# Tridiagonal reduction of a 512 x 512 matrix on one core: reordered steps for three and four remaining tiles, filled pauses for one

## The reference, cut to what matters

```
deg = sum(A, 0) + sum(A, 1) - diagonal(A);  d = rsqrt(deg)
L_norm = d[:, None] * (diag(deg) - A) * d[None, :]
_, U = eigh(L_norm)
h = relu(einsum('mn,bnd->bmd', U.T, x) @ W1 + b1)
x = layernorm(x + einsum('nm,bmd->bnd', U, h @ W2 + b2))
```

## Time and profile before

| | |
|---|---|
| runs (us) | 4988.99, 4991.18, 4991.94; median 4991.18 |
| profiled execution: time, span (us) | 4989.5, 4987.7 |
| busy, share of span | PE 51%, weight load 35%, VectorE 81%, ScalarE 23%, GpSimd 6% |
| the 510 steps | first next column (L1096) at 58.9 us, last at 2530.4 us |
| chain that ended last | VectorE 68%, TensorE 21%, issue 7%, ScalarE 2% |

### The profile page before, as it was taken

One profiled execution on the slowest core, in us unless ns is written; L12 is line 12 of the kernel. 1 busy time (PEld: TensorE's weight loads), 2 busy tenths in 40 slices (PEclk: granted clock), 3 DMA queues, 4 the chain that ended last, 5 costly groups with the idle time before them and its releaser, 6 DMA issues.

```text
span 4987.7 us, 116618 instructions
## 1 busy us (share of the span) xinstructions
PE 2551.1 (51%) x40168; PEld 1721.1 (35%) x40168; DVE 4026.5 (81%) x24921; ACT 1139.3 (23%) x5016; POOL 284.9 (6%) x1424
## 2 busy tenths in 40 slices
PE   4666666555556666544457645657423223135048
PEld 3444444444445555433322212322122223124024
DVE  7666666777777888888889999999967897988956
ACT  1212222222223333333311143333210200301001
POOL 1111111111110000000000000000000000000000
PEclk6555555555555555555567767778755555557579
DMA  2000000000000000000000000000000000000001
GB/s 69 2 2 2 2 2 2 2 2 2 2 2 3 4 4 4 3 3 2 3 1 1 1 1 1 1 1 1 1 1 0 0 0 0 0 0 1 0 0 34
DMA packets 20961, 20.11 MB, mean 4 GB/s; under 512 B 6544, under 2 KB 16784, under 8 KB 20368
## 3 DMA queue, kind: packets, MB, share of 16 engines
...
## 4 chain that ended last, share of the span: by engine, by line
DVE 68%; PE 21%; issue 7%; ACT 2%; SPq 0%; DVEq 0%; DMA 0%; POOL 0%
PE bank L622 10%; DVE qp L1437 2%; DVE hid L1096 2%; DVE dif L1799 2%; PE bank L593 2%; PE bank L617 2%; DVE pcol L1076 2%; DVE tau_row L1084 2%; DVE qp L1424 2%; DVE gated L1082 2%; DVE ts L1040 1%; DVE yz L1055 1%; ACT ts L358 1%; DVE hid L1085 1%; PE bank L783 1%
## 5 line engine op out<-in xcount | busy, mean ns | idle before, releaser
L622 PE MATMUL bank<-lapw,hid 128*32 128x160 f32 (+3 forms) x10200 | 660.0, 420 | 81.5 <-DVE lapw L1105 58.3
L622 PEld LDWEIGHTS bank<-lapw,hid 128*32 128x32 f32 x10200 | 394.3, 162 | 200.0 <-DVE lapw L1105 79.7
L700 PE MATMUL bank<-hid,rows 128*128 128x512 f32 (+1 forms) x504 | 320.1, 802 | 275.3 <-ACT dif L410 271.9
L586 PE MATMUL bank<-xp,ones 128*32 128x1 f32 x4080 | 146.0, 202 | 458.1 <-DVE xp L1070 240.6
L371 ACT ACTIVATE swap<-vcols 128x4 f32<-128x4 f32 (+3 forms) x510 | 105.7, 207 | 1049.4 <-DVE xp L1070 696.8
L1050 DVE TENSOR_TENSOR yz<-bank,pick 128x128 f32<-128x128 f32 (+3 forms) x510 | 117.6, 231 | 233.7 <-PE bank L622 233.5
L700 PEld LDWEIGHTS bank<-hid,rows 128*128 128x128 f32 x504 | 118.7, 242 | 468.1 <-ACT dif L410 297.2
L586 PEld LDWEIGHTS bank<-xp,ones 128*32 128x32 f32 x4080 | 102.6, 140 | 501.4 <-DVE xp L1070 262.2
L593 PE MATMUL bank<-ycol,vcols 128*32 128x1 f32 x3064 | 89.8, 199 | 236.3 <-DVE ycol L1061 236.3
L593 PE MATMUL bank<-hid 128*32 128x1 f32 x3064 | 89.8, 199 | 191.6 <-DVE hid L1096 191.6
L586 PE MATMUL bank<-xn,ones 128*32 128x2 f32 x4080 | 141.2, 198 | 84.1 <-DVE xn L1009 84.1
...
## 6 DMA issues: line engine op xcount, KB each, us to landing
...
hid<-pair SPq DMA_DIRECT2D x32, 1.0 KB, 1.7
...
dif<-in_L_gnn_Wih SPq DMA_DIRECT2D x1, 0.5 KB, 7.1
```

The lines of the kernel that those rows point to most:

```text
L586: m = pe.matmul(into[32 * q:32 * q + 32, :], weights, column, start=True, stop=True)
L622: m = pe.matmul(bank[1][32 * q:32 * q + 32, 0:(T + 1) * 32].rearrange("p (u i) -> p u i", i=32), acols[:, t, k:k + 1].to_broadcast([P, 32] ...
L700: m = pe.matmul(bank[4 * h + q][:, 0:cols_], wih_t[:, p - 1, q * P:(q + 1) * P], hid[:, b0:b0 + nb, t:t + (nw - 1) * p + 1:p], start=True, ...
```

## The change

`dots(k)` becomes two functions, `gated_early(k)` (three or four tiles) and `direct(k)` (one or two); they are each other's opposite.

- Three and four tiles: on VectorE gate_row, gated, tau_row, scrow and ats are issued ahead of the copy of the product (L1050) instead of behind pcol; L1093's product is issued behind bcol_. On TensorE the tail's sum is issued inside the strips, behind the second tile, instead of behind the panel's row. The panel's factor (L1103) is issued ahead of norms(k+1), whose first instruction no longer counts in norm_in.
- One tile: the two instructions on the product are issued behind L1040, and the panel's slots (L1058) behind the second of `pair`.
- All: L1040 waits for the reciprocal (L1037) instead of for L1038, and with one or two tiles the reciprocal is ahead of the wait for alpha. pcol counts in pcol_ready, for which ScalarE waits ahead of w0 and TensorE ahead of the last sum. `product` has its loops exchanged, the tiles outside.

On GpSimd only a branch that no step takes (`t0 == NT - 1`) goes; `tiny` moves in the list of buffers. The core of the diff, ScalarE, TensorE, then VectorE (indented less here):

```
     act.wait_ge(p_ready, k + 1)
-    if dots(k):
+    if direct(k):
         act.activation(ts[:, 7:8], tau_row[:, k:k + 1], ACT.Copy, scale=0.5)
+    act.wait_ge(pcol_ready, k + 1)
     act.activation(w0[:, t0:], pcol[:, t0:], ACT.Copy, scale=tau_row[:, k:k + 1]).then_inc(w0_ready, 1)
...
 def product(into, left, right):
-    for q in range(4):
-        for t in range(T):
+    for t in range(T):
+        for q in range(4):
             m = pe.matmul(into[32 * q:32 * q + 32, :], left[:, t:t + 1].to_broadcast([P, 32]), right[:, t:t + 1], start=(t == 0), stop=(t == T - 1))
...
+    early = gated_early(k)
+    if early:
+        pe.wait_ge(norm_in, k + 1)
+        everywhere(bank[0][:, 0:2], ones[:, 0:32], xn[:, 0:2]).then_inc(norm_ps, 1)
+    else:
         pe.wait_ge(a_ready, k + 1)
         product(bank[0][:, 0:1], acols[:, t0:, k], acols[:, t0:, k]).then_inc(norm_ps, 1)
         everywhere(bank[5][:, 0:1], unit(k), acols[:, t0, k:k + 1]).then_inc(alpha_ps, 1)
-    else:
-        pe.wait_ge(norm_in, 2 * (k + 1))
-        everywhere(bank[0][:, 0:2], ones[:, 0:32], xn[:, 0:2]).then_inc(norm_ps, 1)
...
+        if t == t0 + 1 and early:
+            pe.wait_ge(tail_in, k + 1)
+            everywhere(bank[4][:, 0:1], ones[:, 0:32], xn[:, 2:3]).then_inc(tail_ps, 1)
     m.then_inc(y_done, 1)
     if j:
         everywhere(bank[2][:, 0:2 * j], unit(k), lapw[:, t0, N:N + 2 * j]).then_inc(rowz_ps, 1)
     if k:
         pe.wait_ge(vy_saved, k)
-    pe.wait_ge(tail_in, k + 1)
-    if dots(k):
+    if not early:
+        pe.wait_ge(tail_in, k + 1)
         product(bank[4][:, 0:1], sq[:, 0, t0:], sq[:, 0, t0:]).then_inc(tail_ps, 1)
-        pe.wait_ge(x_ready, k + 1)
+    pe.wait_ge(x_ready, k + 1)
+    if direct(k):
         product(bank[3][:, 0:1], vcols[:, t0:, k], ycol[:, t0:]).then_inc(vy_ps, 1)
-        pe.wait_ge(x2_ready, k + 1)
+        pe.wait_ge(pcol_ready, k + 1)
         product(bank[2][:, 4 * NB:4 * NB + 1], vcols[:, t0:, k], pcol[:, t0:]).then_inc(vp_ps, 1)
     else:
-        everywhere(bank[4][:, 0:1], ones[:, 0:32], xn[:, 2:3]).then_inc(tail_ps, 1)
-        pe.wait_ge(x_ready, k + 1)
         everywhere(bank[3][:, 0:1], ones[:, 0:32], xp[:, 0:1]).then_inc(vy_ps, 1)
         pe.wait_ge(x2_ready, k + 1)
         everywhere(bank[2][:, 4 * NB:4 * NB + 1], ones[:, 0:32], xp[:, 1:2]).then_inc(vp_ps, 1)
...
     dve.wait_ge(a_ready, k + 1)
-    V.tensor_tensor(xn[:, 1:2], acols[:, t0, k:k + 1], ident[:, e:e + 1], ALU.mult).then_inc(norm_in, 1)
+    V.tensor_tensor(xn[:, 1:2], acols[:, t0, k:k + 1], ident[:, e:e + 1], ALU.mult)
     V.tensor_tensor_reduce(jcol[:, 0, t0:], a, a, 1.0, 1e-32, ALU.mult, ALU.add, xn[:, 0:1]).then_inc(norm_in, 1)
...
+    def strips():
+
+        dve.wait_ge(y_done, k + 1)
+        at = put(V.tensor_tensor(yz[:, t0:, 0:32], bank[1][:, 0:T * 32].rearrange("p (t i) -> p t i", i=32),
+                                 pick[:].unsqueeze(1).to_broadcast([P, T, 32]), ALU.mult))
+        if j:
+            dve.wait_ge(w2_ready, k)
+            dve.wait_ge(v2_ready, k)
+            at = put(V.tensor_tensor(yz[:, t0:, 32:32 + 2 * j], panel_cols(j, t0), panel_rows(bank[1][:, T * 32:T * 32 + 32], j, T), ALU.mult))
+        return at
+
+    def slots():
+
+        dve.wait_ge(rowz_ps, rowz)
+        return put(V.tensor_tensor(tz[:, t0:, 1:1 + 2 * j], panel_cols(j, t0), panel_rows(bank[2], j, T), ALU.mult))
+
+    if j:
+        rowz += 1
     dve.wait_ge(norm_root, k + 1)
-    if dots(k):
+    a = put(V.reciprocal(ts[:, 3:4], ts[:, 0:1]))
+    if not early:
         scalars += 1
         dve.wait_ge(alpha_ps, scalars)
-    put(V.reciprocal(ts[:, 3:4], ts[:, 0:1]))
-    a = put(V.tensor_scalar(ts[:, 1:2], alpha, 0.0, 0.5, ALU.is_ge, ALU.subtract))
+    put(V.tensor_scalar(ts[:, 1:2], alpha, 0.0, 0.5, ALU.is_ge, ALU.subtract))
     after(a)
     a = put(V.tensor_scalar(ts[:, 4:5], ts[:, 3:4], bank[0][:, 0:1], ts[:, 0:1], ALU.mult, ALU.add))
+    if T == 1:
+        z = strips()
     after(a)
     a = put(V.tensor_tensor(pair[:, k, 0:1], ts[:, 4:5], ts[:, 1:2], ALU.mult))
     b = put(V.scalar_tensor_tensor(pair[:, k, 1:2], ts[:, 4:5], ts[:, 1:2], alpha, ALU.mult, ALU.add))
+    if T == 1 and j:
+        c = slots()
     after(a)
-    vdone = put(V.scalar_tensor_tensor(v, onehot[:, t0:, k + 1], pair[:, k, 0:1], a_, ALU.mult, ALU.add))
+    put(V.scalar_tensor_tensor(v, onehot[:, t0:, k + 1], pair[:, k, 0:1], a_, ALU.mult, ALU.add))
     after(b)
-    put(V.reciprocal(inv[:], pair[:, k, :]))
-
-    dve.wait_ge(y_done, k + 1)
-    a = put(V.tensor_tensor(yz[:, t0:, 0:32], bank[1][:, 0:T * 32].rearrange("p (t i) -> p t i", i=32),
-                            pick[:].unsqueeze(1).to_broadcast([P, T, 32]), ALU.mult))
-    if j:
-        dve.wait_ge(w2_ready, k)
-        dve.wait_ge(v2_ready, k)
-        a = put(V.tensor_tensor(yz[:, t0:, 32:32 + 2 * j], panel_cols(j, t0), panel_rows(bank[1][:, T * 32:T * 32 + 32], j, T), ALU.mult))
-        rowz += 1
-        dve.wait_ge(rowz_ps, rowz)
-        c = put(V.tensor_tensor(tz[:, t0:, 1:1 + 2 * j], panel_cols(j, t0), panel_rows(bank[2], j, T), ALU.mult))
-    after(a)
-    if dots(k):
-        V.tensor_reduce(ycol[:, t0:], yz[:, t0:, 0:32 + 2 * j], AX.X, ALU.add).then_inc(x_ready, 1)
+    d = put(V.reciprocal(inv[:], pair[:, k, :]))
+    if early:
+        dve.wait_ge(tail_ps, k + 1)
+        g = put(V.tensor_scalar(gate_row[:, k:k + 1], bank[4][:, 0:1], 1e-24, -1.0, ALU.is_gt, ALU.mult))
+        after(g)
+        g = put(V.tensor_scalar(gated[:], inv[:], gate_row[:, k:k + 1], None, ALU.mult))
+        after(g)
+        V.tensor_tensor(tau_row[:, k:k + 1], gated[:, 0:1], gated[:, 1:2], ALU.mult).then_inc(p_ready, 1)
+        dve.wait_ge(p_ready, k + 1)
+        g = put(V.tensor_scalar(scrow[:, k:k + 1], tau_row[:, k:k + 1], gated[:, 0:1], -1.0, ALU.mult, ALU.mult))
+        after(g)
+        put(V.scalar_tensor_tensor(ats[:, t0:], a_, scrow[:, k:k + 1], ltm[:, t0:, k + 1], ALU.mult, ALU.mult))
+    if T > 1:
+        z = strips()
+        if j:
+            c = slots()
+    after(z)
+    y = V.tensor_reduce(ycol[:, t0:], yz[:, t0:, 0:32 + 2 * j], AX.X, ALU.add)
+    if direct(k):
+        y.then_inc(x_ready, 1)
     else:
-        y = put(V.tensor_reduce(ycol[:, t0:], yz[:, t0:, 0:32 + 2 * j], AX.X, ALU.add))
+        y = put(y)
     if j:
         after(c)
     dve.wait_ge(edge_ready, k + 1)
     a1done = put(V.tensor_reduce(a1[:, t0:], tz[:, t0:, 0:1 + 2 * j], AX.X, ALU.add))
-    if not dots(k):
-        after(max(y, vdone))
+    if not early:
+        dve.wait_ge(tail_ps, k + 1)
+        g = put(V.tensor_scalar(gate_row[:, k:k + 1], bank[4][:, 0:1], 1e-24, -1.0, ALU.is_gt, ALU.mult))
+    if not direct(k):
+        after(y)
         V.tensor_tensor_reduce(jcol[:, 1, t0:], v, ycol[:, t0:], 1.0, 0.0, ALU.mult, ALU.add, xp[:, 0:1]).then_inc(x_ready, 1)
-    dve.wait_ge(tail_ps, k + 1)
-    g = put(V.tensor_scalar(gate_row[:, k:k + 1], bank[4][:, 0:1], 1e-24, -1.0, ALU.is_gt, ALU.mult))
     after(a1done)
     if k:
         dve.wait_ge(w0_ready, k)
-    p = V.scalar_tensor_tensor(pcol[:, t0:], a1[:, t0:], pair[:, k, 0:1], ycol[:, t0:], ALU.mult, ALU.add)
-    if dots(k):
-        p.then_inc(x2_ready, 1)
-    else:
-        put(p)
-    after(g)
-    g = put(V.tensor_scalar(gated[:], inv[:], gate_row[:, k:k + 1], None, ALU.mult))
-    after(g)
-    V.tensor_tensor(tau_row[:, k:k + 1], gated[:, 0:1], gated[:, 1:2], ALU.mult).then_inc(p_ready, 1)
+    V.scalar_tensor_tensor(pcol[:, t0:], a1[:, t0:], pair[:, k, 0:1], ycol[:, t0:], ALU.mult, ALU.add).then_inc(pcol_ready, 1)
+    if not early:
+        after(max(d, g))
+        g = put(V.tensor_scalar(gated[:], inv[:], gate_row[:, k:k + 1], None, ALU.mult))
+        after(g)
+        V.tensor_tensor(tau_row[:, k:k + 1], gated[:, 0:1], gated[:, 1:2], ALU.mult).then_inc(p_ready, 1)
+    dve.wait_ge(pcol_ready, k + 1)
     b = put(V.scalar_tensor_tensor(bcol_[:, t0:, k + 1], pcol[:, t0:], gated[:, 0:1], a1[:, t0:], ALU.mult, ALU.add))
-    dve.wait_ge(p_ready, k + 1)
-    c = put(V.tensor_scalar(scrow[:, k:k + 1], tau_row[:, k:k + 1], gated[:, 0:1], -1.0, ALU.mult, ALU.mult))
+    if not early:
+        dve.wait_ge(p_ready, k + 1)
+        c = put(V.tensor_scalar(scrow[:, k:k + 1], tau_row[:, k:k + 1], gated[:, 0:1], -1.0, ALU.mult, ALU.mult))
+    if not direct(k):
+        V.tensor_tensor_reduce(jcol[:, 2, t0:], v, pcol[:, t0:], 0.5, 0.0, ALU.mult, ALU.add, xp[:, 1:2]).then_inc(x2_ready, 1)
     after(b)
     b = put(V.tensor_tensor(bm[:, t0:], bcol_[:, t0:, k + 1], ltm[:, t0:, k + 1], ALU.mult))
-    after(c)
-    c = put(V.scalar_tensor_tensor(ats[:, t0:], a_, scrow[:, k:k + 1], ltm[:, t0:, k + 1], ALU.mult, ALU.mult))
-    if not dots(k):
-        V.tensor_tensor_reduce(jcol[:, 2, t0:], v, pcol[:, t0:], 0.5, 0.0, ALU.mult, ALU.add, xp[:, 1:2]).then_inc(x2_ready, 1)
-    after(c)
+    if not early:
+        after(c)
+        b = put(V.scalar_tensor_tensor(ats[:, t0:], a_, scrow[:, k:k + 1], ltm[:, t0:, k + 1], ALU.mult, ALU.mult))
```

(33 more changed lines are left out.)

19 lines of the change are left out of this document (8 added, 11 removed).

## The result

The changed kernel takes 4878.5 us (median of four runs, 4876.9 to 4878.8), the kernel before 4991.6 us in the same comparison: ratio 0.9773, 95% interval 0.9756 to 0.979. That is 113 us less, where 124 were forecast; 4867 was the forecast, 4838 to 4912 its range. The profiled execution has a span of 4876.7 us against 4987.7, 111 us less.

A forecast was written before the change was run, and what follows sets the result against it. With three or four tiles the product's end was taken to bind, with two and one VectorE's dependent instructions. 79 + 5 + 8 + 32 = 124 us off 4989.5, plus 1.7 for the median, gave 4867 us, range 4838 to 4912.

The forecast's parts named there:

- (a) behind yz: Four tiles, VectorE from yz to acols: five instructions leave the path and acols starts 0.46 us sooner.
- (b) acols to slot: Four tiles, acols to panel slot: 0.58 us instead of 0.88 with the factor ahead of the norms, 0.30 us gained.
- (c) the tail inside the strips: Four tiles, TensorE: the tail's eight narrow passes ahead of the product's end cost 0.12 us a step.
- The bound of 0.29: Tail between strips costs its whole block with latency; part of a 23% rival where insertion and three tiles cost more.
- (d) the moved chain: Four tiles: five moved instructions fit VectorE's 1.33 us pause, tying with the product; 0.62 us a step, 79 us in all.
- The sixth rival: Four tiles: VectorE's moved chain is later than the product by 0.3 and eats half the gain; 4905 us, 5%.
- Three tiles: Three-tile steps: VectorE's branch becomes the end; 0.04 us a step gained, 5 us, bounds 0.12 gained and 0.25 lost.
- Two tiles: Two-tile steps: L1040 starts 0.06 us sooner after the reciprocal, 8 us; product()'s loop order nothing, 6 us either way.
- One tile: One-tile steps: earlier L1040 plus work filled into latencies puts the reduction 1.01 behind the reciprocal, not 1.26; 32 us.
- the third rival: TensorE stalls between strips waiting for tail_in from POOL (GpSimd), making the kernel slower; 3%.
- The clock did not rise: Rival: TensorE's clock rises with four tiles and the strips halve; 4831 us, 2%.
- Pauses: Rival that VectorE's pauses cannot be filled: one tile's 32 us and two tiles' 8 us are gone; 4907 us, 4%.

The follow-up runs named there:

- the doubled tail: Changed kernel with, for four tiles only, the tail's four matmuls issued a second time into a bank nothing reads: 4893.7 us.
- the second experiment: Changed kernel with only the panel's factor put back behind norms(k+1): 4935.9 us; four-tile stage 763.0 us, three-tile stage 696.1 us.

## Why the prediction was right

**Total and sign.** Right, 11 us too much. The errors are the terms' sizes, and one sign: the 5 us forecast as a gain with three tiles came as a loss of 5.4. Half of that miss is hidden in the total by the 5.5 us more of two tiles, from a term that was put at nothing; that part is luck.

**Four tiles, (a) behind yz.** yz and acols at the same panel column (a reduction of 128 x 208), first in the kernel before:

```profile
...
628.03 0.29 DVE L1050 TENSOR_TENSOR yz<-bank,pick 128x128 f32<-128x128 f32 x1 [1.33 <-PE bank L622]
...
630.21 0.23 DVE L1096 SCALAR_TENSOR_TENSOR hid<-ats,bank,bm 128x4 f32<-128x4 f32 x1
...
```

Then in the changed kernel, up to the acols at 576.95 that is shown above:

```profile
...
575.19 0.29 DVE L1041 TENSOR_TENSOR yz<-bank,pick 128x128 f32<-128x128 f32 x1
...
```

2.18 us before and 1.76 after. That is 0.42, where 0.46 stood: pcol moves up by 0.04 instead of 0.05, bcol_ starts 0.26 behind pcol instead of 0.24 and bm 0.26 behind bcol_ instead of 0.25, each a little over the forecast. No run undoes this part alone; it is read from the traces.

**(b) acols to slot.** 0.29 for 0.30; put back, it cost 34.6 of the 37 us expected.

**(c) the tail inside the strips.** 0.11 for 0.12, by the doubled tail, and by the strips themselves: 2.47 us from their start to their end with the tail inside (577.84 to 580.31), 2.36 before. The bound of 0.29 and the estimate of 0.40 us from the Trainium skill's "TensorEngine Tiling (Array Packing)", section "Instruction Overhead", are out for passes that stand between wide ones. The page counts matmuls, and the prediction took it for each of the eight passes; taken for the four matmuls it is an estimate of 0.20 us, still above what was measured.

**(d) the moved chain.** It fits the pause as forecast: yz at 3.43 behind acols (576.95 to 580.38), the forecast's number, held by the product. 0.42 + 0.29 - 0.11 = 0.60 a step, 76 us; 75.2 were measured. The sixth rival (the chain is late by 0.3) is out: yz starts 0.07 behind the strips' end, and 0.21 behind ats, where it needs 0.14 with three tiles. The chain has some 0.07 us to spare, which is little: the tie was forecast.

**Three tiles.** The mechanism was right: the pause of 0.48 us doesn't hold the chain, VectorE becomes the end and the step gains nothing. Its balance came out as +0.04 us a step instead of -0.04. The forecast's own terms gave -0.08, of which it took half. The main term that failed is the norm's start, 0.74 behind acols (1072.35 to 1073.09) where 0.67 stood; the norm's matmul to yz is 0.40 longer in the mean where 0.37 stood, and (a) gave 0.45 where 0.46 stood. The norm starts late because the first norm instruction stands 0.19 behind the factor and not 0.12, and the factor 0.26 behind acols and not 0.23. The eight steps with a panel update lost 0.23 us each, 1.8 of the 5.4 us: the norm is done before the update, as the prediction says, but gate then waits for the tail, which the prediction doesn't name. The prediction also said that of the slot's 0.30 us nothing shows here. As a gain that holds, but the second experiment has its other half: had the slot stayed late, the tail would have been late with it and the stage 24 us slower.

**Two tiles.** 13.5 for 8. L1063's start gave 6.8 (0.053 us a step for 0.06); the loops of product() gave 6.5, which the prediction left at nothing within 6 either way, for want of a row.

**One tile.** 28.4 for 32. yz stands 0.20 behind L1063 (2301.59 to 2301.79), not 0.12; that pushes the first of `pair` 0.07 behind the moment that L1063's end allows, so the reduction comes at 1.08 instead of 1.01 (1.06 in the mean over the stage). pcol then follows the reduction 0.03 us sooner than before, which the prediction didn't count. Of the 28.4 the fills gave 20.9 and L1063's start 6.7, which leaves 0.8. The product was in time: its strips end at 2301.20 + 0.44 and are seen some 0.07 later, at 2301.71, just ahead of yz.

**The other rivals.** TensorE's wait for GpSimd doesn't bind in the change, but the margin of 0.46 us that the prediction worked out was wrong: it took the moment at which the tail's matmuls are due, and TensorE asks with the weight load ahead of them, at 1.71 us behind acols in the mean and not at 2.06. What is left is about 0.05 us with four tiles. That the third rival stayed away is in part luck. The clock did not rise. The changed kernel's granted clock over the whole loop is 0.50, the 1.2 GHz level, with TensorE busy for 1376 of 2420 us:

```profile
...
core 0: us, PE busy (x) PEld busy (x) DVE busy (x) ACT busy (x) POOL busy (x), PEclk, DMA share, GB/s
0.00:2420.00 2420.00, 1376.24 (x36868) 1072.26 (x36870) 1956.51 (x13632) 639.64 (x3903) 278.16 (x1417) 0.50 0.02 6
...
```

**Pauses.** The Trainium skill, "VectorE: DVE Perf Modes", section "The DRAIN you can't avoid", in its strict form would have given one tile nothing from the fills; 20.9 us say otherwise, and agree with its addition that an instruction that isn't held starts earlier.

What stays open: what makes the 0.19 us behind the factor, and why the order of the loops in product() matters.
